# Two layers on 64 small graphs: the hand-written order of the first two turns, changed

## The chip, the cores and the metric

The kernel runs on one core of one Trainium2 chip. The metric is device time in microseconds of one execution, the median of three. An execution is also profiled, and what is read from the profile below is from that one.

## What is computed

A batch of 64 graphs with 128 nodes and 256 features goes through a transformer layer with 8 heads and an edge bias, and then through a single-head attention layer with a layer norm behind it. Everything is float32. The layers, cut to what matters:

```python
# layer 0
nx = _ln(x, ln1_g, ln1_b)
q, k, v = heads(nx @ wq + bq), heads(nx @ wk + bk), heads(nx @ wv + bv)
bias = where(adj > 0, 0.1 * adj * adj, -inf)
attn = softmax(einsum('bhqd,bhkd->bhqk', q, k) / sqrt(32) + bias)
x1 = x + (merge(einsum('bhqk,bhkd->bhqd', attn, v)) @ wo + bo)
x2 = x1 + gelu(_ln(x1, ln2_g, ln2_b) @ w1 + b1) @ w2 + b2
# layer 1
sc = where(adj == 0, -inf, einsum('bld,bmd->blm', x2 @ Wq, x2 @ Wk) / sqrt(256))
y = x2 + (softmax(sc) @ (x2 @ Wv)) @ Wo + bo
out = layer_norm(y, gamma, beta)
```

## The kernel before

The graphs are worked on in groups: group 0 and group 16 have two graphs, groups 1 to 15 have four. Within a group the heads go in pairs of graphs: `q` is the pair (0 or 1), and `r` (0 to 3) one of four PSUM banks, each with four 128x128 score tiles.

Every float32 product that must be exact enough is three products of split operands: a rounded high half, which ScalarE writes (`nxT_copy`, `attn_high`, the second step of `gelu`), and the low rest, which VectorE writes (`nxT_low`, `attn_low`, `h_low`). So nearly every stage goes TensorE, ScalarE, VectorE, TensorE.

The kernel is a pipeline of turns. In a turn one group (`gp`) goes through norm1, projections, scores and softmax, the one before it (`ga`) through attend, output projection and norm2, the one before that (`gb`) through the MLP and layer 1, and the oldest (`gc`) through the last norm. The turns of groups 4 to 15 are one hardware loop; the first and the second turn (groups 2 and 3 as `gp`) are written out by hand, once for each engine, in `first_turn` and `second_turn`. The order of the calls there is the order of each engine's instructions; each call waits on semaphores for what it needs, and what stands behind a waiting call waits too.

The calls that are named later:

- `norm_transpose(3)`, `nxT_copy(3)`, `nxT_low(3)`, `project_k(3, m)`: TensorE transposes the normed input of group 3 into banks 0 and 1 (it waits until all exponentials of group 2 have read them), ScalarE and VectorE split it, TensorE projects.
- `scores(g, q)`, `biased(g, q, r)` (L1363, adds the edge bias and takes the maximum; four instructions for each `r`), `exps(g, q, r)` (L992, four exponentials with their sums), `inverse(g, q, r)` (L1370, reciprocal of the sums), `normal(g, q, r)` on GpSimd (L1911), `blocks(g, q, r)` (L1386, a transpose of 32x32 blocks into `pT`).
- The other half of that transpose is done by DMA: after the last `blocks` of a pair SyncE stores `pT` to `parked` in HBM in four pieces, and when both pairs of a group are there it loads them back, pair 0 into `pT`, then pair 1 into `p_s`. `attend(g, q)` (L586) waits for that load. All this is in SyncE's one queue, in order.
- `attn_high(g, q)`, `attn_low(g, q)`, `out_project(g, q)`, `residual1(g, q)`: the split of the attended values, the projection and the first residual. The high half of pair 1 is kept in a part of `n2T_hi`. `project_v(3, 0)` waits for `residual1(2, 0)`, since they share a bank.
- `scores1(1)` (L687), `biased1(1)` (L1458), `exps1(1)` (L1056), `p1_transpose(1)`, `p1T_copy(1)`, `attend1(1, q)` (L718): layer 1's attention of group 1. `v_copy(3, 0)` frees the bank of `vo_project(1, 0)`.
- `mlp_up(g, j)` and `mlp_down(g, q)`: from tile 4 on `mlp_up` waits for the low half of the tile four before it, `h_low(g, j - 4)`.

The waits that matter for the order are short:

```python
def blocks(g, q, r):
    dve.wait_ge(pool_p, blocks_done(g, q, r))
def load_blocks(g, q):
    for u in pairs(g):
        sp.wait_ge(park_store[u], 64 * g - 64)
def attend(g, q):
    pe.wait_ge(park_load[q], 16 * g - 16)
def exps1(g):
    act.wait_ge(dve_s1, g + 1)
def norm_transpose(g):
    pe.wait_ge(act_p, 4 * pair0(g))   # for g >= 3
```

## Time and profile before

| what | us |
|---|---|
| median of three executions | 894.96 |
| lowest, highest | 894.94, 897.37 |
| the profiled execution | 897.54 |
| its span, first to last instruction | 895.8 |
| TensorE busy in the span | 859.9 |
| VectorE, ScalarE, GpSimd busy | 681.3, 605.3, 503.5 |
| mean granted TensorE clock | 0.987 of full |

The span counts from the first instruction. The first two turns lie between about 55 and 165 us of it; the loop's first turn begins near 163. "Busy" of TensorE is modelled, since its products are pipelined: the first of a run of products is shown some tenths of a us longer than the distance to the next. In a timeline a bracket at the end of a row gives how long the engine had been idle and what ended it; a row that ends in x8 merges eight instructions.

### The profile page before, as it was taken

Reading aid. Unit: us, or ns where it says so; the run is one execution under the profiler, and the core shown is the slowest. Engines: PE = TensorE matmul, PEld = TensorE weight load, DVE = VectorE, ACT = ScalarE, POOL = GpSimd, SP = SyncE. Lnnn points to the kernel's source line nnn. Section 1 sums busy time; section 2 is a strip of 40 time slices with the busy share of each in tenths; the row PEclk is TensorE's granted clock in tenths of the full one; section 3 lists DMA queues with packets and bytes.
Section 4 is the critical chain, followed back from the end, with each engine's and each line's share of the span. In section 5 each row is a group of like instructions: output and inputs, shape, how many; then the busy total and the mean of one; then the engine's idle time right before and its main releaser. Section 6 shows DMA issues by size and latency. Waiting matters only on the chain.

```text
span 895.8 us, 22038 instructions
## 1 busy us (share of the span) xinstructions
PE 859.9 (96%) x7159; PEld 764.0 (85%) x7159; DVE 681.3 (76%) x2522; ACT 605.3 (68%) x1830; POOL 503.5 (56%) x374
## 2 busy tenths in 40 slices
PE   8899898799999999999999999999999999999896
PEld 8787687598898989889898988989898988989795
DVE  6685757878787887868788787878788787875736
ACT  5684854867857676776768676786866678584542
POOL 3522843647667474766657575666757476655312
PEclk9899999999999999999999999999999999999998
DMA  8000231533325242323415241431524233243001
GB/s 270 18 21 13 72 107 62 152 123 90 129 49 173 70 164 82 102 97 81 159 52 176 70 144 63 105 133 47 176 70 164 64 90 120 58 148 114 25 1 36
DMA packets 106304, 87.11 MB, mean 97 GB/s; under 512 B 3462, under 2 KB 91164, under 8 KB 106268
## 3 DMA queue, kind: packets, MB, share of 16 engines
q1 hardware_dynamic: 106252, 86.66, 31.6%
q8 instruction: 19, 0.31, 0.1%
q14 instruction: 17, 0.14, 0.0%
q10 hardware_dynamic: 16, 0.00, 0.0%
HBM read 47.85 MB, written 38.80 MB: 97 GB/s over the span
## 4 chain that ended last, share of the span: by engine, by line
PE 74%; DVE 5%; ACT 4%; issue 3%; POOL 3%; DMA 1%; SPq 0%; DVEq 0%; POOLq 0%; ACTq 0%
PE bank L401 20%; PE bank L403 19%; PE bank L402 19%; PE bank L562 3%; PE bank L687 3%; PE bank L586 3%; PE bank L718 3%; ACT p L1056 2%; DVE p L1458 1%; PE bank L668 1%; PE bank L497 1%; POOL p_s L1911 1%; DMA p_s<-parked 1%; DVE bank L1363 1%; DMA parked<-pT 1%
## 5 line engine op out<-in xcount | busy, mean ns | idle before, releaser
L992 ACT ACTIVATE p_s<-bank,neg_max 128x128 f32<-128x128 f32 x464 | 162.8, 393 | 78.8 <-DVE neg_max L1363 78.8
L1911 POOL TENSOR_TENSOR p_s<-p_s,rsum 128x512 f32<-128x512 f32 x116 | 118.2, 1040 | 91.3 <-DVE rsum L1370 70.9
L401 PE MATMUL bank<-w_hi,hT_hi 128*128 128x256 f32 x512 | 147.5, 288 | 1.2 <-DVE hT_lo L1255 1.2
L403 PE MATMUL bank<-w_hi,hT_lo 128*128 128x256 f32 x512 | 144.0, 281 | 0.0
L402 PE MATMUL bank<-w_lo,hT_hi 128*128 128x256 f32 x512 | 144.0, 281 | 0.0
L1363 DVE CUSTOM_DVE_ANT_0 bank<-bank,bias 128x128 f32<-128x128 f32 x464 | 117.3, 328 | 2.2 <-PE bank L562 2.2
L401 PE MATMUL bank<-n2T_hi,w_hi 128*128 128x512 f32 (+1 forms) x272 | 109.0, 401 | 5.3 <-DVE hT_lo L1255 5.2
L1023 ACT ACTIVATE bank<-bank,vec_cols 128x512 f32<-128x512 f32 (+1 forms) x136 | 86.6, 637 | 33.6 <-PE bank L403 28.0
L992 ACT ACTIVATION_READ_ACCUMULATOR p_s<-bank,neg_max 128x1 f32 x464 | 108.1, 233 | 0.0
L403 PE MATMUL bank<-n2T_hi,w_lo 128*128 128x512 f32 (+1 forms) x272 | 103.7, 381 | 0.0
L402 PE MATMUL bank<-n2T_lo,w_hi 128*128 128x512 f32 (+1 forms) x272 | 103.6, 381 | 0.0
L401 PEld LDWEIGHTS bank<-w_hi,hT_hi 128*128 128x128 f32 x512 | 96.3, 188 | 5.4 <-DVE hT_lo L1255 2.2
L1255 DVE TENSOR_TENSOR hT_lo<-bank,hT_hi 128x512 fp32r<-128x512 f32 (+1 forms) x136 | 85.3, 653 | 17.3 <-ACT hT_hi L928 16.6
L402 PEld LDWEIGHTS bank<-w_lo,hT_hi 128*128 128x128 f32 x512 | 96.4, 188 | 0.0
L403 PEld LDWEIGHTS bank<-w_hi,hT_lo 128*128 128x128 f32 x512 | 96.4, 188 | 0.0
L1897 POOL TENSOR_TENSOR x<-x,bo_r 128x1024 f32<-128x1024 f32 (+1 forms) x16 | 37.4, 2336 | 97.4 <-PE bank L668 97.4
L1822 POOL TENSOR_TENSOR rstd<-ve,minus_half 128x4 f32<-128x4 f32 (+1 forms) x49 | 50.0, 1020 | 70.5 <-DVE ve L1324 68.2
L928 ACT ACTIVATE hT_hi<-bank 128x512 fp32r<-128x512 f32 (+1 forms) x136 | 78.0, 574 | 5.4
L1386 DVE STREAM_TRANSPOSE pT<-p_s 128x512 f32<-128x512 f32 x116 | 78.0, 694 | 3.2 <-POOL p_s L1911 2.9
L1363 DVE DVE_READ_ACCUMULATOR2_ANT neg_max<- 128x1 f32 x512 | 69.7, 136 | 0.0
L401 PEld LDWEIGHTS bank<-n2T_hi,w_hi 128*128 128x128 f32 x272 | 51.4, 189 | 17.5 <-DVE hT_lo L1255 7.7
L403 PEld LDWEIGHTS bank<-n2T_hi,w_lo 128*128 128x128 f32 x272 | 51.2, 188 | 10.6
(237 smaller groups left out, 2430.9 us busy)
## 6 DMA issues: line engine op xcount, KB each, us to landing
parked<-pT SPq DMA_DIRECT2D x116, 256.0 KB, 4.4
pT<-parked SPq DMA_DIRECT2D x15, 1024.0 KB, 5.6
p_s<-parked SPq DMA_DIRECT2D x14, 1024.0 KB, 7.7
xs<-in_x SPq DMA_DIRECT2D x15, 512.0 KB, 4.2
out<-y SPq DMA_DIRECT2D x14, 512.0 KB, 2.9
adj_i<-in_adj SPq DMA_DIRECT2D x15, 256.0 KB, 2.8
out<-y SPq DMA_DIRECT2D x3, 256.0 KB, 2.2
x2T_f<-in_L_gnn_w SPq DMA_DIRECT2D x1, 512.0 KB, 6.8
```

The costliest lines, as they stand in the source:

```text
L401: mm(out, a_hi, b_hi, start=first, stop=False)
L402: mm(out, a_hi, b_lo, start=False, stop=False)
L403: return mm(out, a_lo, b_hi, start=False, stop=last)
L928: return run(dst, src, ACT.Identity, **kw)
L992: last = run(to, of, ACT.Exp, scale=-1.0, bias=neg_max[:, r, place:place + 1], accum_out=psum[:, r, place:place + 1])
L1023: run(h, h, ACT.Gelu, bias=cols["b1"][:, j:j + 1]).then_inc(act_h, 1)
L1255: return V.tensor_tensor(dst, src, hi.bitcast(f32), ALU.subtract)
L1363: last = V.tensor_tensor_reduce(scored if by_blocks(g) else p_s[:, r, place, :], scored, bias0[:, 2 * q + place // 2, :], -1.0, -3.0 * MAS ...
L1386: V.transpose(pT[:, r, :, :].rearrange("p b (l i) -> p l b i", l=4), p_s[:, r, :, :].rearrange("p l (b j) -> p l b j", j=32)).then_inc(dve ...
L1822: P.tensor_tensor(t["rstd"][:, 0:k], t["ve"][:, 0:k], minus_half[:, 0:k], ALU.pow).then_inc(ln_pool[n], 1)
L1897: P.tensor_tensor(x[:, 0:k, :], x[:, 0:k, :], row_of("bo1", k), ALU.add).then_inc(pool_x2b, 1)
L1911: P.tensor_tensor(p_s[:, r, :, :], p_s[:, r, :, :], rsum[:, r, :, None].to_broadcast([128, 4, NODES]), ALU.mult).then_inc(pool_p, 1)
```

## The change

Only the order of calls inside `first_turn` and `second_turn` changes, on TensorE, ScalarE and VectorE. GpSimd's and SyncE's programs stay the same, and so do the loop and the end. In the first turn layer 1's biased scores go ahead of group 2's, the first exponentials of group 2 behind the copies of the n2 and p1 transposes, and one block of scores behind `n2T_low`. In the second turn the low halves of the hidden layer go ahead of block transposes, the norm1 transposes of group 3 go between the two graphs of `mlp_down(1, 1)`, with their low half ahead of the last block transpose, and layer 1's scores of group 1 go between the two attends, with their biased scores and exponentials.

```diff
--- before.py
+++ after.py
@@ -809,8 +809,9 @@
                     mlp_up(1, j, True)
                 scores(2, 1)
                 mlp_down(1, 0)
-                mlp_down(1, 1)
+                mlp_down(1, 1, (0,))
                 norm_transpose(3)
+                mlp_down(1, 1, (1,))
                 project_k(3, 0)
                 project_k(3, 1)
                 x2_transpose(1)
@@ -818,12 +819,12 @@
                 project_q(3, 1)
                 t_project(1)
                 attend(2, 0)
+                scores1(1)
                 attend(2, 1)
                 scores(3, 0)
                 out_project(2, 0)
                 out_project(2, 1)
                 project_v(3, 0)
-                scores1(1)
                 vo_project(1, 0, True)
                 vo_project(1, 1, True)
                 scores(3, 1)
@@ -1130,12 +1131,12 @@
                 t_copy(0)
                 exps1(0)
                 vo_copy(0)
-                exps(2, 0, 0)
                 n2T_copy(1)
                 p1T_copy(0)
+                exps(2, 0, 0)
                 exps(2, 0, 1)
+                v_copy(2, 1)
                 exps(2, 0, 2)
-                v_copy(2, 1)
                 exps(2, 0, 3)
 
             def second_turn():
@@ -1155,6 +1156,7 @@
                 q_copy(3, 1)
                 t_copy(1)
                 attn_high(2, 0)
+                exps1(1)
                 attn_high(2, 1)
                 exps(3, 0, 0)
                 exps(3, 0, 1)
@@ -1162,7 +1164,6 @@
                 v_copy(3, 0)
                 exps(3, 0, 3)
                 vo_copy(1)
-                exps1(1)
                 exps(3, 1, 0)
                 n2T_copy(2)
                 p1T_copy(1)
@@ -1627,13 +1628,14 @@
                 t_copy(0)
                 sums2(1, 1)
                 moments(2, 1)
+                biased1(0)
                 biased(2, 0, 0)
-                biased1(0)
                 norm2(1)
                 inverse_sums1(0)
-                for r in range(1, HPT):
-                    biased(2, 0, r)
+                biased(2, 0, 1)
+                biased(2, 0, 2)
                 n2T_low(1)
+                biased(2, 0, 3)
                 residual3(0, 0)
                 for r in range(HPT):
                     inverse(2, 0, r)
@@ -1641,14 +1643,14 @@
             def second_turn():
                 sums1(3)
                 moments(1, 3)
+                h_low(1, 0)
                 blocks(2, 0, 0)
+                h_low(1, 1)
+                norm1(3)
                 blocks(2, 0, 1)
-                h_low(1, 0)
-                norm1(3)
-                h_low(1, 1)
+                h_low(1, 2)
                 blocks(2, 0, 2)
                 blocks(2, 0, 3)
-                h_low(1, 2)
                 sums3(0)
                 h_low(1, 3)
                 moments(3, 0)
@@ -1664,20 +1666,23 @@
                     inverse(2, 1, r)
                     if r:
                         blocks(2, 1, r - 1)
+                nxT_low(3)
                 blocks(2, 1, 3)
                 residual2(1, 1)
-                nxT_low(3)
                 x2T_low(1)
                 t_copy(1)
                 attn_low(2, 0)
+                biased1(1)
                 attn_low(2, 1)
-                for r in range(HPT):
-                    biased(3, 0, r)
+                biased(3, 0, 0)
+                biased(3, 0, 1)
+                residual1(2, 0, True)
+                biased(3, 0, 2)
+                biased(3, 0, 3)
+                residual1(2, 1, True)
                 inverse(3, 0, 0)
-                residual1(2, 0, True)
                 inverse(3, 0, 1)
                 blocks(3, 0, 0)
-                residual1(2, 1, True)
                 sums2(2, 0)
                 sums2(2, 1)
                 inverse(3, 0, 2)
@@ -1685,13 +1690,14 @@
                 inverse(3, 0, 3)
                 blocks(3, 0, 1)
                 norm2(2)
-                biased1(1)
                 vo_copy(1)
                 blocks(3, 0, 2)
                 blocks(3, 0, 3)
-                for r in range(HPT):
-                    biased(3, 1, r)
+                biased(3, 1, 0)
+                biased(3, 1, 1)
                 n2T_low(2)
+                biased(3, 1, 2)
+                biased(3, 1, 3)
                 inverse_sums1(1)
                 for r in range(HPT):
                     inverse(3, 1, r)
```

On TensorE, the attends of group 2 (`pT` and `p_s` are the two pairs) and, further on, the place that layer 1's scores (L687) left:

```order
 L403 MATMUL bank<-x2T_hi,qk_lo 128x512
 L586 MATMUL bank<-pT,v 32x128 x16
+L687 MATMUL bank<-x2T_f,tT 128x128 x8
 L586 MATMUL bank<-p_s,v 32x128 x16
 L562 MATMUL bank<-kT,qT 128x128 x16
...
 L403 MATMUL bank<-wv_hi,nxT_lo 128x256
-L687 MATMUL bank<-x2T_f,tT 128x128 x8
 L401 MATMUL bank<-vo_hi,x2T_hi 128x256
```

The scores of layer 1 moved from behind the values' projection of group 3 to between the two attends.

On VectorE, the end of the block transposes of group 2's pair 1, before:

```order
L1386 STREAM_TRANSPOSE pT<-p_s 128x4x4x32
L1370 RECIPROCAL rsum<-psum 128x4
L1386 STREAM_TRANSPOSE pT<-p_s 128x4x4x32 x2
L1440 TENSOR_TENSOR x2<-bank5,x1_b2 128x512
L1255 TENSOR_TENSOR nxT_lo<-bank0,nxT_hi 128x512
L1255 TENSOR_TENSOR nxT_lo<-bank1,nxT_hi 128x512
```

and now:

```order
L1371 RECIPROCAL rsum<-psum 128x4
L1387 STREAM_TRANSPOSE pT<-p_s 128x4x4x32
L1256 TENSOR_TENSOR nxT_lo<-bank0,nxT_hi 128x512
L1256 TENSOR_TENSOR nxT_lo<-bank1,nxT_hi 128x512
L1387 STREAM_TRANSPOSE pT<-p_s 128x4x4x32
L1441 TENSOR_TENSOR x2<-bank5,x1_b2 128x512
```

Both halves of `nxT_low(3)` now stand ahead of the last block transpose of the group.

On ScalarE, from the copy of layer 1's t to the last exponentials of group 3's pair 0 (`avT_hi` and `n2T_hi` on banks 6 and 7 are `attn_high` of the pairs), before:

```order
L1049 ACTIVATE tT<-bank4 128x512
L928 ACTIVATE avT_hi<-bank6 128x512
L928 ACTIVATE n2T_hi<-bank7 128x512
L992 ACTIVATE p_s,psum<-bank0,neg_max 128x128 x4
L992 ACTIVATE p_s,psum<-bank1,neg_max 128x128 x4
L992 ACTIVATE p_s,psum<-bank2,neg_max 128x128 x4
L928 ACTIVATE v<-bank6 128x512
L992 ACTIVATE p_s,psum<-bank3,neg_max 128x128 x4
L1061 ACTIVATE vo<-bank6 128x512
L1056 ACTIVATE p1,sum1<-p1,neg_max1 128x128 x4
```

and now:

```order
L1050 ACTIVATE tT<-bank4 128x512
L929 ACTIVATE avT_hi<-bank6 128x512
L1057 ACTIVATE p1,sum1<-p1,neg_max1 128x128 x4
L929 ACTIVATE n2T_hi<-bank7 128x512
L993 ACTIVATE p_s,psum<-bank0,neg_max 128x128 x4
L993 ACTIVATE p_s,psum<-bank1,neg_max 128x128 x4
L993 ACTIVATE p_s,psum<-bank2,neg_max 128x128 x4
L929 ACTIVATE v<-bank6 128x512
```

Layer 1's exponentials moved from behind all exponentials of the pair to between the two `attn_high`.

## Rows read from the trace of the kernel before

**Rows 1.** The page: busy us and share of TensorE, and reloads of p_s.
```profile
PE 859.9 (96%) x7159; PEld 764.0 (85%) x7159; DVE 681.3 (76%) x2522; ACT 605.3 (68%) x1830; POOL 503.5 (56%) x374
...
p_s<-parked SPq DMA_DIRECT2D x14, 1024.0 KB, 7.7
```

**Rows 2.** Chain of waits: start us, us, what; 97 to 140 us.
```profile
97.58 2.14 POOL p_s L1911 x3
...
118.11 4.00 POOL p_s L1911 x4
...
122.14 0.72 DVE pT L1386
...
124.44 4.54 DMA parked<-pT
...
129.52 8.13 DMA p_s<-parked
...
137.69 1.12 PE bank L586 x32
...
138.84 0.61 ACT n2T_hi L928
```

**Rows 3.** Timeline of TensorE: start, us, instructions, [idle before <- releaser].
```profile
90.16 1.06 PE L608 MATMUL bank<-ident,nx 128*128 128x128 f32 x8 [1.17 <-DVE nx L1331]
...
124.75 0.50 PE L401 MATMUL bank<-nxT_hi,wk_hi 128*128 128x512 f32 x1 [1.57 <-DVE nxT_lo L1255]
...
134.59 1.08 PE L586 MATMUL bank<-pT,v 128*32 128x128 f32 x32
...
144.97 0.36 PE L401 MATMUL bank<-wv_hi,nxT_hi 128*128 128x256 f32 x1 [2.05 <-DVE x L1408]
...
146.59 3.43 PE L687 MATMUL bank<-x2T_f,tT 128*128 128x128 f32 x16
...
159.71 0.54 PE L718 MATMUL bank<-vo,p1T 128*128 128x256 f32 x1 [2.46 <-ACT p1T L1065]
...
171.24 0.51 PE L401 MATMUL bank<-n2T_hi,w_hi 128*128 128x512 f32 x1 [2.11 <-DVE hT_lo L1255]
...
210.13 2.02 PE L687 MATMUL bank<-x2T_f,tT 128*128 128x128 f32 x16
```

**Rows 4.** Timeline of ScalarE, first turn and layer 1's exponentials.
```profile
90.02 0.35 ACT L992 ACTIVATE p_s<-bank,neg_max 128x128 f32<-128x128 f32 x1
...
91.39 1.09 ACT L928 ACTIVATE n2T_hi<-bank 128x512 fp32r<-128x512 f32 x2
...
97.45 1.28 ACT L1142 ACT_TABLE_LOAD   x1
...
100.71 0.60 ACT L928 ACTIVATE hT_hi<-bank 128x512 fp32r<-128x512 f32 x1
...
153.80 0.40 ACT L1056 ACTIVATE p<-p,neg_max 128x128 f32<-128x128 f32 x1 [1.72 <-DVE neg_max L1458]
```

**Rows 5.** Timeline of VectorE in the second turn.
```profile
102.71 1.38 DVE L1331 TENSOR_SCALAR nx<-xs,mv,rstd 128x256 f32<-128x256 f32 x4 [1.26 <-issue]
...
121.14 0.71 DVE L1386 STREAM_TRANSPOSE pT<-p_s 128x512 f32<-128x512 f32 x1 [0.23 <-POOL p_s L1911]
...
123.40 1.29 DVE L1255 TENSOR_TENSOR nxT_lo<-bank,nxT_hi 128x512 fp32r<-128x512 f32 x2
...
151.54 1.38 DVE L1331 TENSOR_SCALAR nx<-x,mv,rstd 128x256 f32<-128x256 f32 x4 [1.65 <-POOL rstd L1822]
...
152.84 0.28 DVE L1458 CUSTOM_DVE_ANT_0 p<-bank,pen 128x128 f32<-128x128 f32 x1
```

**Rows 6.** Windows: us, busy (x instructions) of PE, PEld, DVE, ACT, POOL; PEclk, DMA, GB/s.
```profile
140.00:150.00 10.00, 7.95 (x54) 7.77 (x54) 9.29 (x50) 6.29 (x33) 3.70 (x4) 0.83 0.01 2
...
161.00:163.00 2.00, 1.94 (x6) 1.17 (x4) 0.30 (x2) 2.00 (x12) 1.97 (x2) 0.50 0.82 239
...
177.00:200.00 23.00, 23.00 (x255) 20.69 (x254) 16.77 (x74) 15.50 (x53) 13.16 (x10) 1.00 0.40 136
```

## The prediction

> **What bounds the kernel now.** I read the page first: TensorE is busy 96% of the span [rows 1], so work on it is not what can be saved; only its waits can. I then read the chain of waits, because it says which wait ends last in the stretch that the change touches, about 85 to 175 us. There the chain is hardly on TensorE at all [rows 2]: it runs from GpSimd's normalising products of group 2 (97.58) over its next block at 118.11 to VectorE's last block transpose of that group (122.14), from there through the store to `parked` (landed at 124.44 + 4.54) and the reload of `p_s` (129.52 + 8.13) to `attend(2, 1)` at 137.69, then the copy of its result (138.84), and over VectorE, GpSimd and ScalarE to the low half that TensorE waits for before 171.24 [rows 3]. The TensorE timeline [rows 3] shows where that engine idles: 1.57 us before 124.75, 2.05 before 144.97, 2.46 before 159.71, 2.11 before 171.24. From 177 to 200 us it is busy 23.00 of 23 [rows 6], so what the stretch loses is carried to the end one to one, and what TensorE only waits less inside the stretch is worth nothing unless the chain is shortened too. The question for each moved piece is therefore: does it stand ahead of, or behind, a member of that chain on its engine?
>
> The profiled execution took 897.54 us (span 895.8, 1.7 around it); the median of the three timed ones is 894.96, with one at 897.37. I sum changes against the profiled one and add the sum to 894.96.
>
> **The change, part by part.** No instruction is added or removed; every cost is one of place.
>
> *First turn, ScalarE.* Before, the four exponentials `exps(2, 0, 0)` ran at 90.02 to 91.39, a hole in which ScalarE otherwise waits for the n2 transposes of 90.16 [rows 3, 4]. Now they stand behind `n2T_copy(1)` and `p1T_copy(0)`. The hole stays: the copies need the first transposed half, which by the order of the timeline is there about 0.6 us after the transposes start, and these start about 0.35 later, because layer 1's biased scores now go first on VectorE and wait for `scores1(0)`. So the copies start at about 91.14 instead of 91.39, 0.25 sooner, and 1.37 us of exponentials come behind them: ScalarE reaches the table load at 97.45 - 0.25 + 1.37 = 98.57, 1.12 later. TensorE gains 0.25 at `project_v(2, 1)`, which the next wait (for the first low half of the hidden layer) eats.
>
> *Second turn, VectorE's low halves ahead of the block transposes.* This is meant for that next wait, and gives much of it back. `hT_hi` of tile 1 is done at 100.71 + 0.60 + 1.12 = 102.43 [rows 4]; with one block transpose in between `h_low(1, 1)` starts at about 102.5, and `norm1(3)` at 103.15, against 102.71 before [rows 5]. `norm1(3)` releases GpSimd's adjacency work, and that the reciprocal root that `norm3(0)` waits for, so **+0.44** passes on to the scores of group 2 and to GpSimd's products at 118.11. TensorE's up projection ends about 0.3 later: it is not on the chain.
>
> *norm1 transposes inside the MLP.* TensorE loses nothing (the same eight transposes, 1.0 us) and gains the wait of 1.57 before `project_k(3, 0)` [rows 3], so it arrives some 1.1 us sooner at `attend(2, 0)`. But `nxT_low(3)`, 1.29 us on VectorE [rows 5], now stands ahead of `blocks(2, 1, 3)`. The block before that starts at 121.14 and ends at 121.78, the last one at 122.14 after a wait for GpSimd; with the 0.44: 122.22 + 1.25 = 123.47 instead of 122.14, **+1.33** in all (0.44 + 0.89). Store and both reloads follow that transpose, so `pT` and `p_s` land 1.33 later. `attend(2, 0)` started at 134.59 [rows 3], which was already the landing of `pT` within 0.4 us; it goes to 135.92, and the 1.1 us that TensorE gained become a wait of 2.5 us there.
>
> *Layer 1's scores between the attends.* `attend(2, 0)` takes 1.08, to 137.0. `scores1(1)` at full clock takes 2.02 (at 210.13, [rows 3]; 0.27 of it tail), to 138.75; `p_s` lands at about 138.9, so `attend(2, 1)` is only 0.1 us later than its data let it be. The trouble is behind it. On ScalarE `exps1(1)` stands ahead of `attn_high(2, 1)`, and on VectorE `biased(3, 0, 0)` stands behind `attn_low(2, 1)`. The biased scores of layer 1 run at 138.8 to 139.65 (four, 0.85 us, [rows 5]), the exponentials from 139.77 for 4 x 0.39 = 1.56 [rows 4], so `attn_high(2, 1)` starts at 141.33 instead of 138.84: **+2.5** for the first scores of group 3.
>
> *Behind them.* Both residual adds now stand ahead of the first reciprocal (about 0.65 each, which is what one of the two equally wide steps of `nxT_low` takes, [rows 5]); one of them was ahead of the reciprocals' consumers anyway, so `norm2(2)`, at 151.54 before, comes 0.6 later against the scores. The four biased scores of layer 1 (0.85 us) no longer stand between `norm2(2)` and the scores of the second pair. Net -0.2, and the exponentials, the residuals and block transposes after them up to `h_low(2, 0)` are the same chain as before. `project_v(3, 0)` no longer waits 2.05 for the residual after the scores, but its copy stands behind the exponentials, and `vo_project` has lost the layer-1 scores that covered it: TensorE waits about 1.7 there, and about 3 before the n2 transposes. All of that is beside the chain.
>
> Sum without any change of the clock: 2.5 - 0.2 = **+2.3 us** at the up projection of 171.24.
>
> **The clock.** TensorE's granted clock was 0.83 in 140 to 150 us and 0.50 in 161 to 163 [rows 6], that is the lower level (1.2 GHz), in each case behind the waits of 2.05 and 2.46 us; behind the wait of 2.11 the first product took 0.51 (171.24), as at 124.75 (0.50), so there it stayed at 2.4 GHz. In the kernel before these falls cost nothing, for the chain ran elsewhere: `scores1(1)` at 146.59 took 3.43 instead of 2.02. In the changed kernel the wait of 2.5 us stands right ahead of `attend(2, 0)` and `scores1(1)`, which are now the chain. If the clock falls there, **+1.4** (3.43 - 2.02), bounds 0 and 1.7 (the second with part of the attend slow as well). The stall of some 3 us before the up projection near 173 could cost up to 0.7 more in the same way.
> On this the Trainium skill (TensorE: Matmul & The Clock Gate, section HAM oscillation) has a rule of thumb for the idle gap that is harmless which would let 2.5 us pass; by it the sum stays at +2.3. The trace speaks against it, with a fall behind 2.05. The same page (What's actually happening) says that the gate doesn't restart with the kernel, so the same gap may fall either way from one execution to the next; three waits of about one size, two with a fall and one without, agree.
>
> **The rivals.**
> A, my forecast: the chain as above, with the lower clock behind the wait: 2.3 + 1.3 = +3.6, **898.5 us**. For it: every member is in the chain view. Against: it needs the clock to fall.
> B: the same chain, clock stays up: +2.3, 897.3 us.
> C, the reloads land early: what is late at `blocks(2, 1, 3)` is made good in the DMA. The reload of `p_s` took 8.13 here and its median over the kernel is 7.7 [rows 1], so some 0.4 is to be had there and perhaps 0.2 in the stores: B becomes +1.7, and if the exponentials of layer 1 also fit before `attend(2, 1)`'s end, +0.5: 895.5 to 896.7 us.
> D, the other side: TensorE's own waits are what counts, because ScalarE and VectorE have slack that the chain view hides (a wait there is only put down to one engine). Place: the two waits of 1.57 and 2.05 at `project_k(3, 0)` and `project_v(3, 0)`. Price: -3.6, and +0.3 for the later end of the up projection, -3.3: 891.7 us. It decides if the first scores of group 3 start before 140.1. Against it: `attend(2, 0)` already waited for DMA.
> E: the pieces add up worse, both falls of the clock and another at `vo_project`: +4.3 to +5.5, up to 900.5 us.
>
> **How the numbers follow.** A 0.40, B 0.27, C 0.15, D 0.08, E 0.10. A measurement of this kernel can tell 0.3% from no change, 2.7 us. C is wholly within; B (+2.3, with half a us of my own error and a spread of 2.4 us among the three runs) is within in some 7 of 10; A is beyond in about 8 of 10. Faster 0.07, same 0.41, slower 0.52. The range leaves out D and the far end of E: from 895.0 (the good end of C, with a little spread) to 900.5.
>
> **What would show it.** Right: ScalarE's table load near 98.6; `blocks(2, 1, 3)` near 123.5; `project_k(3, 0)` without a wait near 123.7; a new wait of 2 to 2.5 us for DMA before `attend(2, 0)` near 135.9; `attn_high(2, 1)` behind `exps1(1)`, near 141.3 or up to 1.4 later; the n2 transposes of group 2 waiting for `norm2`, some 3 us; the first wait in the loop's first turn near 173.5. Wrong: if `attend(2, 0)` starts before 135, or if `attn_high(2, 1)` doesn't wait for the exponentials. The whole falls if the loop absorbs it: then TensorE's first full stretch would start later but the last matmul would not.

## The result, and the profile of the changed kernel

The changed kernel took 899.85 us (median of six, 898.82 to 901.31) against 895.40 (six, 894.85 to 897.37) for the one before: ratio 1.0048, 95% interval 1.0034 to 1.0061, so it is 4.4 us slower. The forecast was 898.5 us, +3.5 on the median of three known then (894.96); the median of all six executions before is 895.40. The ratios and intervals here and below are those on record with each run; they are not the quotients of the two medians beside them and differ from these by up to 0.0016.

The page answers [rows 1] with the same busy times within 2.1 us and the same reload, so nothing became more work:

```profile
PE 858.5 (96%) x7159; PEld 762.2 (85%) x7159; DVE 679.5 (76%) x2522; ACT 607.4 (68%) x1830; POOL 503.3 (56%) x374
...
p_s<-parked SPq DMA_DIRECT2D x14, 1024.0 KB, 7.7
```

The chain of waits of the changed kernel (start us, us, what), which answers [rows 2]:

```profile
119.91 0.71 DVE pT L1387
120.63 1.17 DVE nxT_lo L1256 x2
121.80 0.63 DVE pT L1387
...
124.00 4.54 DMA parked<-pT
...
128.60 5.75 DMA pT<-parked
...
134.40 1.93 PE bank L586 x32
136.33 2.53 PE bank L687 x16
...
140.34 1.35 ACT p L1057 x7
141.69 0.49 ACT n2T_hi L929
```

`nxT_low(3)` stands between the last two block transposes, and behind the reload of `pT` come the first attend, layer 1's scores and their exponentials, all ahead of `attn_high(2, 1)`. Before, the reload of `p_s` and the second attend stood there.

TensorE's timeline, for [rows 3] (start, us, instructions, idle before and its releaser in brackets):

```profile
118.44 1.06 PE L497 MATMUL bank<-ident,nx 128*128 128x128 f32 x8 [0.39 <-ACT p_s L993]
...
134.40 1.93 PE L586 MATMUL bank<-pT,v 128*32 128x128 f32 x32 [2.38 <-DMA pT<-parked]
136.26 2.59 PE L687 MATMUL bank<-x2T_f,tT 128*128 128x128 f32 x16
138.78 1.08 PE L586 MATMUL bank<-p_s,v 128*32 128x128 f32 x32
...
148.81 0.39 PE L401 MATMUL bank<-vo_hi,x2T_hi 128*128 128x256 f32 x1 [1.56 <-ACT v L929]
...
156.31 1.06 PE L608 MATMUL bank<-ident,nx 128*128 128x128 f32 x8 [3.29 <-DVE nx L1332]
...
173.67 0.51 PE L401 MATMUL bank<-n2T_hi,w_hi 128*128 128x512 f32 x1 [1.05 <-DVE hT_lo L1256]
```

`project_k(3, 0)` no longer waits. The wait of 2.38 us ahead of `attend(2, 0)` is new, and behind it the attend takes 1.93 us instead of 1.08. Before, TensorE waited one attend later, for the second reload, and the attend behind that wait ran at full speed:

```profile
137.69 1.08 PE L586 MATMUL bank<-p_s,v 128*32 128x128 f32 x32 [2.02 <-DMA p_s<-parked]
```

ScalarE, for [rows 4], and VectorE, for [rows 5]:

```profile
96.97 1.28 ACT L1143 ACT_TABLE_LOAD   x1
...
140.03 0.40 ACT L1057 ACTIVATE p<-p,neg_max 128x128 f32<-128x128 f32 x1 [3.04 <-DVE neg_max L1459]
...
141.60 0.57 ACT L929 ACTIVATE n2T_hi<-bank 128x512 fp32r<-128x512 f32 x1
```

```profile
101.49 1.37 DVE L1332 TENSOR_SCALAR nx<-xs,mv,rstd 128x256 f32<-128x256 f32 x4
...
120.55 1.25 DVE L1256 TENSOR_TENSOR nxT_lo<-bank,nxT_hi 128x512 fp32r<-128x512 f32 x2
121.72 0.69 DVE L1387 STREAM_TRANSPOSE pT<-p_s 128x512 f32<-128x512 f32 x1
```

Windows (us, busy and instructions of PE, PEld, DVE, ACT, POOL, then granted clock, DMA share, GB/s), for [rows 6]:

```profile
125.00:135.00 10.00, 7.48 (x45) 5.69 (x47) 2.08 (x3) 4.80 (x8) 2.41 (x1) 0.95 0.76 237
135.00:140.00 5.00, 5.00 (x80) 4.21 (x75) 1.62 (x9) 0.60 (x1) 0.00 (x0) 0.76 0.59 194
...
180.00:200.00 20.00, 20.00 (x232) 17.78 (x230) 13.93 (x56) 14.02 (x46) 12.60 (x10) 1.00 0.41 144
```

The granted clock was 0.76 in 135 to 140, part of it at the lower level of 1.2 GHz, and from 180 us on TensorE is full again.

**How the executions are compared.** The profiled execution took 899.99 us (span 898.2), only 2.45 more than that of before. But it had reached `scores(2, 0)` at 83.43 us instead of 85.31, in code that the change does not touch. So I count every event from one common event of the same execution: from `scores(2, 0)` to `norm1(3)`, and from `norm1(3)` on. The same code took 17.40, 17.41, 17.75 and 18.50 us from the first to the second in four kernels (before, o1_norm, k1_fillbefore, p1_biaslate). The granted clock tells these apart. It was 1.00 from 90 to 97 us in the first two and lower in the others (before, k1_fillbefore, p1_biaslate, in this order; columns as above):

```profile
90.00:97.00 7.00, 5.47 (x34) 4.85 (x35) 5.31 (x33) 7.00 (x36) 6.67 (x4) 1.00 0.28 78
```

```profile
90.00:97.00 7.00, 5.87 (x26) 5.37 (x27) 4.37 (x23) 6.76 (x29) 6.44 (x5) 0.76 0.29 80
```

```profile
90.00:97.00 7.00, 5.88 (x20) 5.23 (x21) 3.62 (x21) 6.75 (x29) 5.69 (x5) 0.53 0.28 78
```

At the lower clock layer 1's attend of group 0 ends later, and GpSimd's products of group 2 then wait 0.32 and 1.07 us for VectorE's reciprocals behind it. The kernels with the changed first turn divide in the same way: 17.95 to 18.08 us in five traces without a low stretch that begins at 90 to 91 us (f1_first, after, u2_scores1back, g1_attnfirst, c1_both), 18.48 to 18.56 in three with one (u1_lowlast, w1_fill, w2_fill10). The prelude shows it too: the five traces with a low stretch near 10 us (the one of before among them) reach `scores(2, 0)` at 85.16 to 85.31 us, six that lack it, but have the later ones near 22 and 39 us, at 83.32 to 83.63. From 5 to 15 us the clock was 0.83 before and 1.00 in the changed kernel. So the first distance has to be compared between traces of like clock; before and after are such a pair. From `norm1(3)` on, the end of the stretch in k1_fillbefore, whose chain is as in the kernel before, differs by 0.08.

Absolute times would have misled. The prediction's sign of being wrong was an `attend(2, 0)` before 135 us, and rival D's a first product of group 3's scores before 140.1. The changed kernel shows 134.40 and 139.79; with the 1.88 us by which it was ahead at `scores(2, 0)` they are 136.28 and 141.67.

| shift against before, from `norm1(3)` | after | u1_lowlast | u2_scores1back | w2_fill10 | g1_attnfirst | o1_norm | f1_first | c1_both | b1_short |
|---|---|---|---|---|---|---|---|---|---|
| `blocks(2, 1, 3)` | +0.80 | 0.00 | +0.81 | +0.80 | +0.79 | +0.82 | +0.01 | -0.02 | +0.20 |
| `attend(2, 0)` | +1.03 | +0.09 | +0.86 | +0.96 | +0.89 | +0.94 | +0.19 | +0.14 | +0.30 |
| `attend(2, 1)` | +2.31 | -0.02 | +0.72 | +2.19 | +2.21 | +0.90 | +0.20 | +0.03 | +0.19 |
| `attn_high(2, 1)` | +3.98 | +1.64 | +1.57 | +2.52 | +2.37 | +1.76 | +0.30 | +0.03 | +0.19 |
| `norm2(2)` | +4.46 | +2.13 | +3.00 | +3.00 | +2.92 | +2.67 | +1.24 | +0.59 | -0.89 |
| up projection (171.24 in [rows 3]) | +3.65 | +1.31 | +3.02 | +2.17 | +2.07 | +2.67 | +1.24 | -0.27 | -1.14 |
| the same, from `scores(2, 0)` | +4.31 | +2.39 | +3.66 | +3.32 | +2.75 | +2.68 | +1.79 | +0.34 | -1.89 |

The last row of the first column, +4.31, is close to the measured +4.45, and what was lost by the up projection near 173 us was carried to the end: from there the span has 724.56 us left before and 724.53 after.

### The profile page after: what moved, and what is told of

It is laid out like the page before. It is cut to its first block, busy times and chain, and to the rows that moved or that the text cites. A ratio compares the mean times of both kernels' runs of the same rounds, so it can differ in the third digit from the quotient of the medians.

```text
span 898.2 us, 22038 instructions
## 1 busy us (share of the span) xinstructions
PE 858.5 (96%) x7159; PEld 762.2 (85%) x7159; DVE 679.5 (76%) x2522; ACT 607.4 (68%) x1830; POOL 503.3 (56%) x374
## 4 chain that ended last, share of the span: by engine, by line
PE 74%; DVE 5%; ACT 3%; POOL 3%; issue 2%; DMA 1%; SPq 0%; DVEq 0%; POOLq 0%; ACTq 0%
PE bank L401 20%; PE bank L403 19%; PE bank L402 19%; PE bank L687 3%; PE bank L562 3%; PE bank L586 3%; PE bank L718 3%; ACT p L1057 2%; POOL p_s L1917 1%; DVE p L1459 1%; PE bank L668 1%; PE bank L497 1%; DVE bank L1364 1%; DMA pT<-parked 1%; DMA parked<-pT 1%
## 5 line engine op out<-in xcount | busy, mean ns | idle before, releaser
L1364 DVE DVE_READ_ACCUMULATOR2_ANT neg_max<- 128x1 f32 x512 | 72.6, 142 | 0.0
```

The costliest lines, as they stand in the source:

```text
L1364: last = V.tensor_tensor_reduce(scored if by_blocks(g) else p_s[:, r, place, :], scored, bias0[:, 2 * q + place // 2, :], -1.0, -3.0 * MAS ...
```

## The experiments

Each time is given beside runs of the kernel before on the same chip, in three sets. Their medians are 896.47 (u1, u2, w1, p1), 896.15 (w2, g1, o1, b1) and 896.16 (k1, f1, c1, b2). The executions of one kernel differ by several us, and their mean granted clock differs with them. In the third set the five at 0.986 or less took 897.37 to 900.53 us, the eight at 0.991 or more 894.60 to 895.58.

### Where the loss is: one place undone at a time

**u1_lowlast**, the changed kernel with the low half of the norm1 transposes behind the last block transpose:

```diff
 # second_turn, VectorE
-                nxT_low(3)
                 blocks(2, 1, 3)
+                nxT_low(3)
```

> The changed kernel with one thing undone: nxT_low(3) stands behind blocks(2, 1, 3) on VectorE again. Theory (the chain through the block transposes, the reloads and layer 1's exponentials is the bound): the last block transpose of group 2 comes 0.9 us earlier, both reloads and all behind them too: 0.9 less than the changed kernel, +3.5 against the kernel before (about 899). Rival (TensorE's own waits are the bound): project_k(3, 0) waits again for about 1 us and the time stays or rises by 1.

897.84 us, ratio 1.0014 (0.9991 to 1.0036), where I had expected about 899. TensorE's timeline of u1_lowlast:

```profile
134.04 1.08 PE L586 MATMUL bank<-pT,v 128*32 128x128 f32 x32 [0.67 <-DMA pT<-parked]
135.05 2.05 PE L687 MATMUL bank<-x2T_f,tT 128*128 128x128 f32 x16
```

The reload comes 0.9 us sooner, and TensorE arrives 0.8 later (the projection waits for its low half again), so the wait shrinks from 2.38 to 0.67. The clock then stays up: attend 1.08, scores 2.05. From `norm1(3)` on the edit gives 2.3 us, not the 0.9 that the place alone costs; the rest is the clock, for from the first attend to the second it is now 2.99 us instead of 4.38. What is left, +1.3, is the place of the exponentials.

**u2_scores1back**, the changed kernel with layer 1's scores, biased scores and exponentials where they were:

```diff
 # second_turn, TensorE; the same for biased1(1) (VectorE), exps1(1) (ScalarE)
                 attend(2, 0)
-                scores1(1)
                 attend(2, 1)
...
                 project_v(3, 0)
+                scores1(1)
```

> The changed kernel with layer 1's scores, their biased scores and exponentials back in the places of before, on all three engines; all else stays. Theory: attend(2, 1) still starts 1.3 us late with its reload, but nothing of layer 1 stands ahead of attn_high(2, 1) and a lower clock in the wait costs nothing; behind it 0.6 for the residuals. +1.9 against before (about 897.3), 2.4 less than the changed kernel. Rival (only the lower clock costs): 1.5 less, +2.9. Rival (the scores' place doesn't matter, the first turn and the low half do): no difference from the changed kernel.

900.46 us, ratio 1.0029 (1.0008 to 1.0049), no better than what the changed kernel showed within the error; the stretch is 0.6 shorter. TensorE's timeline of u2_scores1back:

```profile
136.06 1.94 PE L586 MATMUL bank<-pT,v 128*32 128x128 f32 x32 [2.22 <-DMA pT<-parked]
...
139.02 1.93 PE L586 MATMUL bank<-p_s,v 128*32 128x128 f32 x32 [1.02 <-DMA p_s<-parked]
140.88 2.03 PE L562 MATMUL bank<-kT,qT 32*128 32x128 f32 x32
```

I had expected about 897.3, +1.9. Of the chain only `attn_high(2, 1)` came as early as expected; the wait of 2.22 us remained, and now both attends and the scores of group 3 (2.03 instead of 1.17) ran at the lower clock, on the chain (1.17 is what the changed kernel's scores took at full clock). So the fall is not bound to layer 1's scores: it taxes whatever stands behind the wait.

**g1_attnfirst**, the changed kernel with only ScalarE's two pieces exchanged:

```diff
 # second_turn, ScalarE
                 attn_high(2, 0)
-                exps1(1)
                 attn_high(2, 1)
+                exps1(1)
```

> The changed kernel with exps1(1) behind attn_high(2, 1) on ScalarE; all else as changed. Theory: attn_high(2, 1) follows attend(2, 1) at once, 1.2 to 1.7 us earlier, and the scores of group 3 on VectorE with it; the exponentials of layer 1 fit before the first ones of group 3 are ready but for some 0.3 us. 1.3 us less than the changed kernel, +2.8 against before. Rival (the four exponentials only change places with a wait): no difference.

899.06 us, ratio 1.0034 (1.0023 to 1.0045). The stretch is 1.6 us shorter than in the changed kernel, as the 1.57 us of exponentials ask for, while the clock still fell: behind a wait of 2.31 the attend took 1.08, but layer 1's scores 3.48. Attend and scores together took 4.42 us here and 4.38 in the changed kernel, where the attend was slow as well. At full clock the two took 2.99 us (u1_lowlast, w1_fill, c1_both), so their sum, 1.4 us more, is a sounder measure of the clock's price than the one or the other.

### Does the clock fall cost what it seems to?

**w1_fill** and **w2_fill10** keep TensorE busy in the wait, with products of the identity that nobody reads:

```diff
 # second_turn, TensorE; warm(20) in w1_fill
                 t_project(1)
+                pe.wait_ge(act_q, 8)
+                warm(10)
                 attend(2, 0)
```

> The changed kernel with 20 products of the identity with itself into bank 0 ahead of attend(2, 0), some 2.2 us of added work on TensorE in the wait for the reload; their result is not used. Theory (the lower clock behind that wait costs 1.5 of the 4.1 us): attend(2, 0) and scores1(1) take 2.8 instead of 4.4 us and the time falls by up to 1.5 us (less on average if the clock does not fall in every execution), 898.4 to 899. Rival (the clock costs nothing, the order does all): the same as the changed kernel, 899.9. Rival (TensorE is the bound): slower by up to 2.

I had sized w1_fill wrong: each product is two instructions, so 20 took 4.63 us instead of the 2.2 that were wanted, and `attend(2, 0)` came 2 us late. 901.31 us, ratio 1.0047 (1.0028 to 1.0067). It says only that the clock stays up there (attend 1.08, scores 2.05).

> The changed kernel with 10 products of the identity ahead of attend(2, 0). Twenty of them took 4.6 us and held attend(2, 0) up by 2 us, while the clock stayed at 1.00; ten take 2.3 us and end before the reload lands. Theory (the lower clock costs 1.5 us on attend(2, 0) and scores1(1)): attend(2, 0) at its data, 1.08 + 1.8 us for the two, attn_high(2, 1) 1.5 earlier, 1 to 1.5 us less than the changed kernel, +2.5 to +3 against before. Rival (order alone): the same as the changed kernel.

With 10, TensorE's timeline of w2_fill10:

```profile
132.28 2.39 PE L462 MATMUL bank<-ident 128*128 128x128 f32 x20
134.78 1.08 PE L586 MATMUL bank<-pT,v 128*32 128x128 f32 x32
135.79 2.05 PE L687 MATMUL bank<-x2T_f,tT 128*128 128x128 f32 x16
...
139.11 1.08 PE L586 MATMUL bank<-p_s,v 128*32 128x128 f32 x32 [1.26 <-DMA p_s<-parked]
```

With the attend where it was (+0.96 for +1.03) both attends and the scores ran at full speed, and `attn_high(2, 1)` came 1.46 us sooner, the stretch's end 1.48. That is the price of the clock in the profiled execution, measured on the chain. One thing differs besides: the reload of `p_s` took 9.5 us from issue to landing instead of 8.1, so `attend(2, 1)` is hardly sooner (+2.19 for +2.31). `attn_high(2, 1)`, which stands behind layer 1's exponentials, did not wait for it. The price agrees with the 1.4 us of g1_attnfirst and u1_lowlast. The median is 899.42 us, ratio 1.0043 (1.0028 to 1.0057), which can't be told from the changed kernel's. So the trace shows the price of one fall, not how many executions have it, and the expected 1 to 1.5 us are not shown in the time.

**k1_fillbefore** asks the same of the kernel before, which waits about 2 us ahead of `attend(2, 1)`:

```diff
 # before: second_turn, TensorE
                 attend(2, 0)
+                pe.wait_ge(act_q, 8)
+                warm(8)
                 attend(2, 1)
```

> The kernel before with 8 products of the identity (1.84 us) between attend(2, 0) and attend(2, 1), in the wait of 2.0 us for the second reload. Theory: in some executions of the kernel before the clock falls behind that wait and attend(2, 1) and scores(3, 0), which are in the chain, take up to 1.7 us more; with the wait filled it doesn't fall. The median falls by 0.3 to 1.2 us and the executions spread less at the top. Rival: no difference, or +0.1 where the reload lands early.

896.19 us (894.70 to 898.17), ratio 0.9995 (0.9982 to 1.0009). The expected gain of 0.3 to 1.2 us is not shown. The highest times are lower than those of before beside it (up to 900.53), but twelve runs don't settle that: inconclusive.

### One part of the change, added to the kernel before

**o1_norm**, the norm1 transposes inside the MLP alone. This is the test of rival D, since it takes away the wait of 1.57 us at `project_k(3, 0)` and lays only VectorE's 1.25 us on the chain:

```diff
 # before: second_turn, TensorE, VectorE
-                mlp_down(1, 1)
+                mlp_down(1, 1, (0,))
                 norm_transpose(3)
+                mlp_down(1, 1, (1,))
...
+                nxT_low(3)
                 blocks(2, 1, 3)
                 residual2(1, 1)
-                nxT_low(3)
```

> The kernel before with the norm1 transposes of group 3 inside mlp_down(1, 1) and nxT_low(3) ahead of blocks(2, 1, 3), nothing else. Theory: TensorE starts project_k(3, 0) about 1.5 us earlier, but the last block transpose of group 2 ends 0.9 later and with it both reloads and all behind: +0.9 against before. Rival (TensorE's waits are the bound): 1.5 less than before.

899.28 us, ratio 1.0040 (1.0024 to 1.0056). TensorE was 1.37 us sooner at `project_k(3, 0)`, and the kernel is 0.4% slower: D is refuted. The timeline of TensorE and a window (columns as in the windows above) of o1_norm show more:

```profile
132.91 1.45 PE L586 MATMUL bank<-pT,v 128*32 128x128 f32 x32 [2.32 <-DMA pT<-parked]
...
135.97 1.94 PE L586 MATMUL bank<-p_s,v 128*32 128x128 f32 x32 [1.61 <-DMA p_s<-parked]
137.84 2.09 PE L562 MATMUL bank<-kT,qT 32*128 32x128 f32 x32
```

```profile
134.00:138.00 4.00, 2.39 (x44) 1.54 (x36) 0.69 (x1) 0.62 (x2) 0.00 (x0) 0.50 0.65 217
```

The time that TensorE saved became a wait of 2.32 us, and at 0.50 of the clock the second attend and the scores behind it took 1.94 and 2.09 instead of 1.08 and 1.17. The first half of that, +0.9 at `attn_high(2, 1)`, and the second, +0.9 at the scores, made +0.9 into +2.7. I had expected +0.9: the miss is the clock again.

**f1_first**, the first turn's change alone (all of `first_turn` of the changed kernel on ScalarE and VectorE):

```diff
 # before: first_turn, ScalarE (the move of v_copy(2, 1) and VectorE's part as in the change)
-                exps(2, 0, 0)
                 n2T_copy(1)
                 p1T_copy(0)
+                exps(2, 0, 0)
```

> The kernel before with the first turn's part of the change alone. Theory: ScalarE reaches the table load 1.1 us later, but norm1(3) on VectorE waits for GpSimd's root until 102.7 us anyway and the two block transposes ahead of the first low half cover the rest, so the chain moves by 0 to 0.2: between no difference and +0.3 against before; the +0.44 of the changed kernel came from the low halves ahead of norm1(3). Rival (what ScalarE loses is lost): +1.1.

898.33 us, ratio 1.0021 (1.0004 to 1.0038): slower, where I had expected no difference to +0.3. The table load comes 13.50 us behind `scores(2, 0)` instead of 12.14, and `norm1(3)` 0.55 later. VectorE of f1_first:

```profile
102.15 0.64 DVE L1255 TENSOR_TENSOR hT_lo<-bank,hT_hi 128x512 fp32r<-128x512 f32 x1
103.11 1.38 DVE L1331 TENSOR_SCALAR nx<-xs,mv,rstd 128x256 f32<-128x256 f32 x4 [0.32 <-issue]
```

VectorE is still idle 0.32 us ahead of `norm1(3)`, so what ScalarE and VectorE do just before it does not hold it up. GpSimd's reciprocal root does. GpSimd's first work of the stretch (`x` plus the output bias) and the root, before and then in f1_first:

```profile
90.10 2.35 POOL L1881 TENSOR_TENSOR x_bo<-xs,bo_r 128x1024 f32<-128x1024 f32 x1 [1.75 <-DVE nx L1331]
...
101.54 1.04 POOL L1822 TENSOR_TENSOR rstd<-ve,minus_half 128x4 f32<-128x4 f32 x1
```

```profile
90.48 2.35 POOL L1882 TENSOR_TENSOR x_bo<-xs,bo_r 128x1024 f32<-128x1024 f32 x1 [2.29 <-DVE nx L1331]
...
101.94 1.04 POOL L1823 TENSOR_TENSOR rstd<-ve,minus_half 128x4 f32<-128x4 f32 x1
```

In both `norm1(3)` starts 0.13 us behind the root's end. Counted from `scores(2, 0)`, GpSimd's first work and the root are 0.53 and 0.55 us later in f1_first; between them GpSimd has no gap over 0.2 us in either. What it waited for first is `norm2(1)` on VectorE, which is late because `biased1(0)` now stands ahead and waits 0.56 us for `scores1(0)`. The 1.36 us that ScalarE lost are beside this chain. Of the other +1.24 us, 0.2 come with the reload of `pT` and 0.9 between `attn_high(2, 1)` and `norm2(2)`: the clock was 0.50 in 140 to 142 us behind a wait of 2.04, and the scores of group 3 took 2.09 instead of 1.17. The kernel before had such a wait without a fall in its profile.

**p1_biaslate**, GpSimd's adjacency bias of group 3 behind its products of group 2:

```diff
 # before: second_turn, GpSimd
-                bias(3)
                 for r in range(HPT):
                     normal(2, 1, r)
+                bias(3)
```

> The kernel before with one change on GpSimd: bias(3) of the second turn stands behind the four products normal(2, 1, r). It tests the chain where TensorE has no part. Theory: the products start 0.7 us earlier and the last block transpose of group 2 ends about 0.55 earlier, with it the reloads, attend(2, 1) and all behind: 0.5 us less than before. Rival (TensorE's waits or the DMA decide): no difference, the landmarks at attend(2, 1) stay.

896.22 us, ratio 0.9985 (0.9966 to 1.0004), inconclusive for an expected gain of 0.5 us. The last block transpose came 0.59 sooner as expected, but `attend(2, 0)` not at all (TensorE itself arrives no earlier) and `attend(2, 1)` 0.18, since the reload of `p_s` took 8.54 instead of 8.13. TensorE of p1_biaslate:

```profile
136.93 1.08 PE L586 MATMUL bank<-p_s,v 128*32 128x128 f32 x32 [1.84 <-DMA p_s<-parked]
137.94 1.93 PE L562 MATMUL bank<-kT,qT 32*128 32x128 f32 x32
```

Behind 1.84 us of wait the scores ran slow, and the small gain was gone (+0.55 at the stretch's end from `norm1(3)`; from `scores(2, 0)` it is +1.65, with the low clock at 90 us in it).

### Do the two places and the clock make all of it?

**c1_both** undoes both places of the changed kernel and keeps the rest:

```diff
 # second_turn, ScalarE, VectorE
-                exps1(1)
                 attn_high(2, 1)
+                exps1(1)
...
-                nxT_low(3)
                 blocks(2, 1, 3)
+                nxT_low(3)
```

> The changed kernel with both costly places undone: nxT_low(3) behind blocks(2, 1, 3), and exps1(1) behind attn_high(2, 1). Theory: the reloads land as before, TensorE's wait ahead of attend(2, 0) is only some 1.2 us and the clock stays up, scores1(1) fills the wait between the attends; left are 0.4 of the first turn and 0.6 of the residuals, less 0.85 for the biased scores: within 0.5 of before. Rival (the rest of the change costs as well): at least +2.

896.71 us, ratio 0.9997 (0.9983 to 1.0012): the loss is gone. The clock was 1.00 from 134 to 140, attend and scores took 1.08 and 2.05, behind a wait of 0.73. The first turn's change and layer 1's scores between the attends are still in it. The stretch is 3.97 us shorter than in the changed kernel, so nearly all of the loss is these two places and the clock fall that they bring. Of the first turn's +0.6 half is made good by the end (-0.27 from `norm1(3)`, +0.34 in all).

**b1_short** keeps from the change what TensorE gains, and shortens the chain (two reciprocal roots and the bias on GpSimd moved):

```diff
 # before: TensorE as in the change; h_low(1, 0) to (1, 2), norm1(3), biased1(1) and exps1(1)
 # as in c1_both; the first turn and the rest of VectorE as before but for nxT_low(3),
 # which stands ahead of residual2(1, 1)
 # GpSimd, first_turn and second_turn
-                for r in range(HPT):
-                    normal(2, 0, r)
+                normal(2, 0, 0)
+                normal(2, 0, 1)
+                rstd(1, 3)
+                normal(2, 0, 2)
+                normal(2, 0, 3)
...
-                rstd(1, 3)
...
-                bias(3)
                 for r in range(HPT):
                     normal(2, 1, r)
+                bias(3)
                 x2_plus_bo(1)
-                for r in range(HPT):
+                for r in range(3):
                     normal(3, 0, r)
                 rstd(2, 2)
+                normal(3, 0, 3)
```

> The kernel before with what the chain asks for: norm1 transposes inside the MLP but nxT_low(3) behind the last block transpose; scores1(1) between the attends, biased1(1) ahead of attn_low(2, 1), exps1(1) behind attn_high(2, 1); low halves h_low(1, 0) and (1, 1) ahead of block transposes; on GpSimd rstd(1, 3) between the products of group 2, bias(3) behind group 2's second products, rstd(2, 2) ahead of normal(3, 0, 3). Theory, against before: norm1(3) 0.65 earlier, last block transpose 0.55 more, norm2(2) 1.15 more, layer 1's biased scores out of the way 0.85: -3.2, 892 to 893.5 us. Rival (the shortened places are beside the bound): within 1 us of before.

894.69 us, ratio 0.9979 (0.9968 to 0.9990): faster by 1.5 us in the medians and 1.9 by the ratio, not by 3.2. `rstd(1, 3)` let `norm1(3)` start early, 16.65 us behind `scores(2, 0)`, but VectorE and GpSimd of b1_short show what came of it:

```profile
101.94 2.21 DVE L1332 TENSOR_SCALAR nx<-xs,mv,rstd 128x256 f32<-128x256 f32 x4
```

```profile
101.00 2.04 POOL L1912 TENSOR_TENSOR p_s<-p_s,rsum 128x512 f32<-128x512 f32 x2
```

Beside the products it took 2.21 us instead of 1.38, and the last two products themselves came one root later.

**b2_shorter** puts that root back and clears the chain elsewhere:

```diff
 # b1_short: rstd(1, 3) as in before; VectorE
-                norm3(0)
...
                 residual2(1, 1)
+                norm3(0)
...
                 inverse(3, 1, 1)
+                residual3(1, 0)
+                residual3(1, 1)
                 inverse(3, 1, 2)
+                blocks(3, 1, 0)
                 inverse(3, 1, 3)
-                residual3(1, 0)
-                residual3(1, 1)
 # GpSimd
-                gain(0, 2)
-                offset(0, 2)
...
                 bias(3)
+                gain(0, 2)
+                offset(0, 2)
```

> The shortened kernel with three more places: the root of norm1(3) on GpSimd again behind the products of group 2 (beside them norm1(3) took 2.21 instead of 1.38 us); norm3(0) on VectorE and gain and offset of group 0 on GpSimd behind group 2's block transposes, so that the scores of group 2 don't wait for GpSimd's root (1.2 us sooner, of which 0.8 reach attend(2, 1)); residual3(1, q) ahead of inverse(3, 1, 2), in a wait for ScalarE, so that the block transposes and sums1(4) come 1.5 to 2 us sooner. Theory: -4.5 against before, 891.5 us. Rival (the chain moves to TensorE): about the same as the shortened kernel, -1.9.

893.23 us (891.88 to 894.10), ratio 0.9955 (0.9937 to 0.9973). It is the best of all, 2.9 us faster than the kernel before in the medians and 4.0 by the ratio, against -4.5 expected; in the profiles the up projection comes 3.04 us sooner behind `scores(2, 0)`. From `norm1(3)` on, the last block transpose of group 2 is 0.73 sooner, `norm2(2)` 1.79, `attend1(1)` 2.03. TensorE of b2_shorter:

```profile
133.93 1.08 PE L586 MATMUL bank<-pT,v 128*32 128x128 f32 x32 [0.72 <-DMA pT<-parked]
134.94 2.05 PE L687 MATMUL bank<-x2T_f,tT 128*128 128x128 f32 x16
...
170.72 0.50 PE L401 MATMUL bank<-n2T_hi,w_hi 128*128 128x512 f32 x1 [0.93 <-DVE hT_lo L1256]
```

Layer 1's scores between the attends are in this kernel too. With their exponentials behind `attn_high(2, 1)` and the DMA not made late, they fill the wait for `p_s` instead of making one.

## Why the prediction was right

The chain of the second turn came as forecast, member by member, and the size within 0.9 us (+3.5 predicted, +4.4 measured). The first turn's part came with nearly the forecast size, but mostly by another path. By the prediction's own steps:

- **First turn.** Forecast +1.12 at the table load, measured 13.54 - 12.14 = +1.40. The 0.25 us that were to be gained did not come: the n2 transposes start 0.54 later, not 0.35, and in f1_first the copies start only 0.03 sooner. Forecast +0.44 at `norm1(3)`, measured +0.66. In the changed kernel `norm1(3)` does follow `h_low(1, 1)` without a gap, as forecast. But the prediction left out that GpSimd's root was late as well, over `norm2(1)`: it ended 0.54 later against `scores(2, 0)`, which alone gives +0.54 (f1_first, +0.55). ScalarE's exponentials added only 0.12. That the number was near is in part luck.
- **`nxT_low(3)` ahead of the last block transpose.** Forecast +0.89, measured +0.80. The reload of `pT` passed it on with +1.03; o1_norm (+0.82, +0.94) and u1_lowlast (0.00, +0.09) show the place alone, both ways.
- **The wait before `attend(2, 0)`.** Forecast 2.5 us, measured 2.38. `project_k(3, 0)` without a wait: measured.
- **Scores, biased scores and exponentials of layer 1 ahead of `attn_high(2, 1)`.** Forecast +2.5 in all, without the clock. Measured +3.98 behind `norm1(3)` and 0.66 ahead of it, 4.64; without the clock's 1.46, 3.2. The exponentials took their 1.57; what is over is 0.2 in the first turn, 0.1 at the reload, 0.15 between the scores and the first exponential (1.17 us, forecast 1.02), and 0.16 at attend and scores (2.99 us at full clock, planned 2.83).
- **Behind them.** Forecast -0.2, measured 3.65 - 3.98 = -0.33. `norm2(2)` is at first later than that (+4.46); the four biased scores that left its back give it back by `attend1(1)` (+3.62). The n2 transposes waited 3.29 (forecast about 3), `vo_project` 1.56 (1.7).
- **The clock.** Forecast +1.4 (the sum then uses 1.3), bounds 0 to 1.7. Measured 1.46 by w2_fill10; the attend and the scores together took 4.38 us against 2.99 at full clock. The further 0.7 near 173 did not come: the wait there is 1.05, and the product behind it took 0.51. In w2_fill10 the clock did fall there, behind a wait of 2.78 (the product took 0.79), and from there to layer 1's scores near 211 us it took 39.10 us instead of 38.89, so the price was 0.2.
- **A wait left out.** The prediction counts three waits of about 2 us, two with a fall and one without. There is a fourth, the 2.02 us ahead of `attend(2, 1)`, and it is the one that stands on the chain of the kernel before. Behind it the clock stayed up in that profile, and fell in f1_first and p1_biaslate. So the kernel before can lose time to the clock too, and the forecast compares with an execution that did not there.

With the measured terms the sum is 3.18 + 1.46 - 0.33 = 4.31, for a forecast of 2.5 + 1.3 - 0.2 = 3.6. It was too small by 0.7, spread over four small terms; the clock's 0.16 more and the 0.13 less behind cancel.

The rivals: **B** (clock stays up) gives way to **A** in every profile with a wait of 2.2 us or more directly ahead of the first attend; w2_fill10 shows B in the changed order (+3.32 instead of +4.31), u1_lowlast and c1_both show it once the wait is short. That the clock would fall was the right choice on little evidence, 0.40 for A against 0.27 for B. **C** fell: the store landed in 4.54 us as before, the reload of `pT` took 5.75, and the first attend was late by 0.23 more than the transpose (+1.03 for +0.80), not by less. **D** was refuted by o1_norm. **E** named the right direction of the error but not its place: the changed kernel's profile has no fall at `vo_project` or near 173.

On the harmless idle gap the Trainium skill (TensorE: Matmul & The Clock Gate, section HAM oscillation) has a rule of thumb that would let 2.4 us pass. It doesn't protect here: the granted clock fell to 0.50 behind waits of 2.38, 2.32, 2.31, 2.22, 2.04 and 1.84 us. But the length of the wait alone doesn't decide it, for the clock stayed up behind waits of 2.05 (b1_short), 2.11 (before), 2.78 (u2_scores1back) and 2.79 us (c1_both). The same page (What's actually happening) says that the gate does not restart with the kernel; with that a wait of about 2 us ahead of `attend(2, 1)` without a fall in the kernel before, and with one in f1_first, agree.

**What stays open.** How often the clock falls at this place in executions that are not profiled; w2_fill10 and k1_fillbefore, which should have shown it in the medians, did not tell. The mean granted clock of the executions says a little. Its median was 0.984 in o1_norm and u2_scores1back, with none above 0.987, against 0.990 and 0.988 in the kernel before beside them; so in most executions of these two the clock was low for longer. That fits a fall at this place in most of them, but does not show the place. It was 0.987 in the changed kernel and 0.988 in w2_fill10, too near to tell. And it is open why the clock falls behind one wait of about 2 us and not behind another.

## What to carry to other kernels

Before work is moved into an idle gap, ask what the gap waits for and what chain its neighbours on the other engines are members of: here 1.25 us of VectorE and 1.57 us of ScalarE went ahead of chain members, and TensorE's saved 1.3 us only turned into a longer wait. A wait of about 2 us directly ahead of work on the chain can cost more than itself, since the work behind it may run at the lower clock; in the profiles, shortening that wait from 2.4 to 0.7 us was worth 2.3 us where its cause was worth 0.9. And compare two traces by distances from a common event inside each execution, or a difference in the prelude (1.9 us here) hides half of the effect. Look at the granted clock of every stretch that lies between the two events: code that nobody touched took up to 1.1 us longer where it was low.

## What the runs showed of the hardware that I had not expected

Four TENSOR_SCALAR instructions on VectorE (128x256, float32, SBUF to SBUF) took 2.21 us beside two of GpSimd's products in b1_short and 1.36 to 1.38 without them. `norm2(2)`, four instructions of the same shape, took 1.98 beside one product in b1_short and b2_shorter and 1.38 in all the others. The Trainium skill (GPSIMD Engine Reference, section 1. Specifications) says that GpSimd shares its SBUF interfaces with VectorE; the measured 0.83 and 0.60 agree, and give it a size.

A float32 product of two 128x128 tiles is two instructions, 0.23 us together at full clock (4.63 us for 20 of them, 2.39 for 10).

The granted clock did not act at once or at the same point: behind equal waits of 2.38 and 2.31 us the attend took 1.93 in one kernel and 1.08 in the other, and the scores behind it 2.59 and 3.48; only the sum agreed (4.38 and 4.42).
